# Routed attention: scatters two at a time behind each tile's weighing, TensorE's part as a loop, GpSimd filling the ring of rows

## The reference, cut to what matters

```python
x = x + tanh(g_xattn[3]) * L3_xattn(layernorm(x), ctx, ctx, Wq, bq, Wk, bk, Wv, bv, Wo, bo)
x = x + tanh(g_ffn[3]) * L3_ffn(layernorm(x), router_w, w1, b1, w2, b2)

def L3_ffn(x, router_w, w1, b1, w2, b2):          # 8 experts, two for each token
    router_probs = softmax(x_flat @ router_w.T)
    top_k_probs, top_k_idx = lax.top_k(router_probs, TOP_K)
    top_k_probs = top_k_probs / (top_k_probs.sum(-1, keepdims=True) + 1e-08)
    cw = (one_hot(top_k_idx, E) * top_k_probs[..., None]).sum(axis=1)
    for e in range(E):
        output += cw[:, e:e+1] * (new_gelu(x_flat @ w1[e].T + b1[e]) @ w2[e].T + b2[e])
```

## Time and profile before

| | us |
|---|---|
| median of the timed runs | 3279.86 (3278.26 to 3281.05) |
| the profiled execution, its own time | 3298.21 |
| its span in the profile | 3296.4 |
| TensorE busy | 2532.8 (77%) |
| VectorE busy | 1566.6 (48%) |
| ScalarE busy | 1380.2 (42%) |
| GpSimd busy | 978.3 (30%) |

### The profile page before, as it was taken

How to read it: one execution, slowest core, us unless ns; L and a number is a source line. 1 busy time by engine, 2 the same in 40 slices (tenths; PEclk the granted TensorE clock), 3 DMA queues, 4 the chain that set the end, 5 groups by cost and what they waited for, 6 DMA issues and landing times. The chain is left out here.

```text
span 3296.4 us, 74894 instructions
## 1 busy us (share of the span) xinstructions
PE 2532.8 (77%) x28202; PEld 1794.6 (54%) x28202; DVE 1566.6 (48%) x4283; ACT 1380.2 (42%) x1992; POOL 978.3 (30%) x1052
## 2 busy tenths in 40 slices
PE   4888864439997799989999969993288777358883
PEld 2555543328886455567777735551145444247773
DVE  3555544424443577622222247776667665513322
ACT  2555533213332466644545436661055444124441
POOL 4444426634444112110000000001112433634444
PEclk9999976669999899989999979996599888679997
DMA  3010101126665222100000011110011111146666
GB/s 98 22 24 20 23 16 38 39 80 195 197 192 153 78 53 61 34 3 0 0 0 0 1 44 45 41 41 11 11 32 31 37 35 37 44 144 191 189 186 219
DMA packets 143775, 219.56 MB, mean 67 GB/s; under 512 B 27177, under 2 KB 94513, under 8 KB 143026
## 3 DMA queue, kind: packets, MB, share of 16 engines
q1 hardware_dynamic: 96930, 90.25, 10.8%
q10 hardware_dynamic: 29232, 90.37, 8.8%
q0 software_dynamic: 17408, 36.21, 3.2%
HBM read 157.48 MB, written 43.61 MB: 61 GB/s over the span
## 5 line engine op out<-in xcount | busy, mean ns | idle before, releaser
L1541 DVE TENSOR_REDUCE mx<-psS 128x16 f32<-128x1024 f32 x264 | 322.6, 1222 | 321.9 <-PE psS L1096 294.1
L650 POOL DMA_INDIRECT yg<-ysb,yidx x288 | 279.5, 970 | 421.0 <-DVE ysb L2005 190.6
L470 POOL TENSOR_TENSOR ve<-mv,eps 128x4 f32<-128x4 f32 x102 | 20.3, 199 | 1184.4 <-DVE mv L1517 1182.3
L756 ACT ACTIVATE work<-psT 128x1024 f32<-128x1024 f32 x260 | 266.2, 1024 | 215.5 <-PE psT L1105 214.8
L750 ACT ACTIVATE work<-work 128x1024 f32<-128x1024 f32 x264 | 278.3, 1054 | 135.9 <-DVE work L1543 132.7
L1096 PE MATMUL psS<-kexp,qT 64*64 64x512 f32 x2112 | 307.6, 634 | 31.0 <-DMA kexp<-kT 15.3
L1543 DVE TENSOR_TENSOR work<-psS,mx 128x1024 f32<-128x1024 f32 x264 | 323.2, 1224 | 9.1
L1105 PEld LDWEIGHTS psT<-ident,work 128*128 128x128 f32 x2080 | 239.6, 145 | 151.5 <-issue 99.8
L1105 PE MATMUL psT<-ident,work 128*128 128x128 f32 x2080 | 288.3, 283 | 5.3 <-ACT work L756 3.3
L1381 PEld LDWEIGHTS psY<-w_ffn,work 128*128 128x128 f32 x2016 | 247.8, 192 | 9.4 <-DVE work L1976 1.2
L1381 PE MATMUL psY<-w_ffn,work 128*128 128x128 f32 x2016 | 248.5, 275 | 1.6 <-DVE ysb L1999 1.0
(11 more groups left out here) (278 smaller groups left out, 4645.0 us busy)
## 6 DMA issues: line engine op xcount, KB each, us to landing
w_ffn<-in_wmoe ACTq DMA_DIRECT2D x72, 578.0 KB
w_ffn<-in_wmoe ACTq DMA_DIRECT2D x72, 576.0 KB
ctxT<-in_ctxT SPq DMA_DIRECT2D x76, 256.0 KB, 2.8
xin<-xg SPq DMA_DIRECT2D x144, 132.0 KB
kexp<-kT SPq DMA_DIRECT2D x1152, 16.0 KB
gio<-yg SPq DMA_DIRECT2D x16, 512.0 KB, 3.9
work<-yg SPq DMA_DIRECT2D x16, 512.0 KB, 6.4
yg<-ysb,yidx POOLq DMA_INDIRECT x288
```

The lines of the kernel that those rows point to most:

```text
L650: e.indirect_dma_start(out=yg, out_offset=bass.IndirectOffsetOnAxis(ap=yidx[:, b, t:t + 1], axis=0), in_=ysb[:, b, t, :], in_offset=None, ...
L756: e.activation(pT[:, s % 2, :], psT[:, :], ACT.Copy).then_inc(pt_ok, 1)
L1541: e.tensor_reduce(mx[:, :], src, AX, ALU.max).then_inc(s_max, 1)
```

## The change

Three things in `attention_routed(3)`, and what they need elsewhere:

- GpSimd's `scatter(k)` issues two indirect DMAs in place of eight; k runs from 0 to 63. One such pair is issued behind each tile's weighing: `behind_weighing(u, s)` waits for `pv_ps` of tile (u, s). After the last turn the remaining 27 pairs follow in two runs, with the last two norms and fills between them.
- `rows(c)`, new on GpSimd, writes the normalised rows to `ring`. VectorE's `apply` writes the same numbers to a new tile `xnf` of one chunk, from which TensorE transposes. `macc` is one buffer, and VectorE waits for `rank_ps` before it updates it.
- TensorE's program has turns 0 to 3 written out, then a loop of five passes of two turns, then six turns. Its waits take their values from the loop's register where they are inside.

```diff
-                def scatter(g, c):
-                    if c == 0:
+                def rows(c):
+                    b = (c % 2) * LT
+                    if c >= 8 and c % 2 == 0:
+                        e.wait_ge(m[f"sd{c // 2 % 4}"], 16 * 2 * GT * (c // 8))
+                    e.wait_ge(m["rstd"], c + 1)
+                    for t in range(LT):
+                        mm = e.tensor_scalar(ring[c // 2 % 4][:, b + t, 0:D], xs(None, c, t), mmv[:, b + t, 0:1],
+                                             mrstd[:, 1, b + t:b + t + 1], ALU.subtract, ALU.mult)
+                    mm.then_inc(m["nrm"], 1)
+
+                def scatter(k):
+                    g, c, t0 = k // 8, k // 4 % 2, 2 * (k % 4)
+                    if k % 8 == 0:
                         e.wait_ge(m["seq"], MSTEPS[lay] * (g + 1))
-                    for t in range(GT):
+                        e.wait_ge(m["nrm"], 2 * g + 2)
+                    for t in range(t0, t0 + 2):
                         e.indirect_dma_start(
...
+                def behind_weighing(u, s):
+                    k = 4 * (u - 6) + s - 3
+                    if k >= 0:
+                        e.wait_ge(pv_ps, K0 + lay * TILES + u * LT + s + 1)
+                        scatter(k)
...
-                for u in range(CHUNKS + 5):
+                for u in range(CHUNKS):
+                    behind_weighing(u, 0)
                     if u + 2 <= CHUNKS:
                         ln(ATT[lay], None, u + 2)
-                    if 2 <= u < CHUNKS + 2:
+                    if u >= 2:
                         norm(u - 2)
-                    if u < CHUNKS:
-                        x_bias(lay, None, u)
-                    if u >= 6 and u % 2 == 0:
-                        scatter((u - 6) // 2, 0)
-                    if u >= 7 and u % 2 == 1:
-                        scatter((u - 7) // 2, 1)
-                scatter(NG - 1, 1)
+                    x_bias(lay, None, u)
+                    behind_weighing(u, 1)
+                    if u >= 2:
+                        rows(u - 2)
+                    behind_weighing(u, 2)
+                    behind_weighing(u, 3)
+                first = 4 * (CHUNKS - 6) - 3
+                norm(CHUNKS - 2)
+                rows(CHUNKS - 2)
+                for k in range(first, 8 * (NG - 3)):
+                    scatter(k)
+                norm(CHUNKS - 1)
+                rows(CHUNKS - 1)
+                for k in range(8 * (NG - 3), 8 * NG):
+                    scatter(k)
...
-                        mm = e.transpose(psX[:, t * P:(t + 1) * P], ring[c // 2 % 4][:, c % 2 * LT + t, 0:D], ident[:, :])
+                        mm = e.transpose(psX[:, t * P:(t + 1) * P], xnf[:, t, :], ident[:, :])
...
-                for u in range(CHUNKS + 4):
+
+                def turn(i, u):
...
+                for u in range(4):
+                    turn(None, u)
+                with e.Fori(0, (CHUNKS - 6) // 2) as i:
+                    turn(i, 4)
+                    turn(i, 5)
+                for u in range(CHUNKS - 2, CHUNKS + 4):
+                    turn(None, u)
...
                     if c >= 2:
                         e.wait_ge(m["xn"], c - 1)
+                        e.wait_ge(m["nrm"], c - 1)
...
                 def apply(c):
                     b = c % 2 * LT
-                    if c >= 8 and c % 2 == 0:
-                        e.wait_ge(m[f"sd{c // 2 % 4}"], 16 * 2 * GT * (c // 8))
+                    if c >= 1:
+                        e.wait_ge(m["xt_ps"], c)
...
-                        mm = e.tensor_scalar(ring[c // 2 % 4][:, b + t, 0:D], xs(None, c, t), mmv[:, b + t, 0:1],
+                        mm = e.tensor_scalar(xnf[:, t, :], xs(None, c, t), mmv[:, b + t, 0:1],
...
-                    step(e.tensor_tensor, macc[:, lay // 3, (g + 1) % 2, :], macc[:, lay // 3, g % 2, :], mcol[:, 8, :], ALU.add)
+                    e.wait_ge(m["rank_ps"], g + 1)
+                    step(e.tensor_tensor, macc[:, lay // 3, 0, :], macc[:, lay // 3, 0, :], mcol[:, 8, :], ALU.add)
```

More of the change, by code:

```diff
@@ L140, in program @@
         ring.append(gio3[:, :, :])
+        xnf = sb("xnf", [P, LT, D])
         lgt = sb("lgt", [P, GT * E])
@@ L1189, in attention_routed, with turn_x, route @@
                 m = MO[lay]
-                def turn_x(c):
-                    e.wait_ge(m["xn"], c + 1)
-                    e.wait_ge(x_up, K0 + lay * CHUNKS + c + 2 if c + 2 <= CHUNKS else K0 + (lay + 1) * CHUNKS)
+                def turn_x(i, u):
+                    e.wait_ge(m["xn"], val(i, u, 1, -2))
+                    e.wait_ge(x_up, val(i, min(u, CHUNKS + 1), 1, K0 + lay * CHUNKS - 1))
                     for t in range(LT):
-                        mm = e.transpose(psX[:, t * P:(t + 1) * P], ring[c // 2 % 4][:, c % 2 * LT + t, 0:D], ident[:, :])
+                        mm = e.transpose(psX[:, t * P:(t + 1) * P], xnf[:, t, :], ident[:, :])
                     mm.then_inc(m["xt_ps"], 1)
-                def route(c):
-                    e.wait_ge(m["xt_sb"], c + 1)
+                def route(i, u):
+                    e.wait_ge(m["xt_sb"], val(i, u, 1, -2))
                     for t in range(LT):
@@ L1202, in route, with group, rank @@
                     mm.then_inc(m["r_ps"], 1)
-                def rank(g):
-                    e.wait_ge(m["seq"], MSTEPS[lay] * g + 18)
+                def group(i, u, per, plus):
+                    return per * ((u - 5) // 2) + plus if i is None else i * per + (per * ((u - 5) // 2) + plus)
+                def rank(i, u):
+                    e.wait_ge(m["seq"], group(i, u, MSTEPS[lay], 18))
                     out8 = psX[:, GT * E:2 * GT * E].rearrange("p (t x) -> p t x", t=GT)
@@ L1210, in rank @@
                                  start=False, stop=False, skip_group_check=True)
-                    e.matmul(out8, ones16[:, :], macc[:, lay // 3, g % 2, :].rearrange("p (a x) -> p a x", a=1)
+                    e.matmul(out8, ones16[:, :], macc[:, lay // 3, 0, :].rearrange("p (a x) -> p a x", a=1)
                              .broadcast_to([P, GT, E]), start=False, stop=True).then_inc(m["rank_ps"], 1)
@@ L1224, in attention_routed @@
                 p_turn(lay, None, 0, 0)
-                for u in range(CHUNKS + 4):
+                def turn(i, u):
                     inside = u < CHUNKS
-                    c = u - 3
+                    routed = 3 <= u < CHUNKS + 3
+                    ranked = u >= 5 and u % 2 == 1
                     for s in range(LT):
                         if inside:
-                            scores(lay, None, *ahead(u, s, 2))
+                            scores(lay, i, *ahead(u, s, 2))
                         if s == 1 and inside:
[L1232 to L1240, removed]
+                            q_proj(lay, i, u + 1)
+                        if s == 1 and routed:
+                            turn_x(i, u)
+                        if s == 2 and routed:
+                            route(i, u)
+                        if s == 3 and routed:
+                            e.wait_ge(m["lg"], val(i, u, 1, -2))
+                        if s == 3 and ranked:
+                            rank(i, u)
@@ L1241, in attention_routed @@
                         if inside:
-                            p_turn(lay, None, *ahead(u, s, 1))
-                        if s == 3 and u >= 5 and u % 2 == 1:
-                            e.wait_ge(m["rk"], (u - 5) // 2 + 1)
+                            p_turn(lay, i, *ahead(u, s, 1))
+                        if s == 3 and ranked:
+                            e.wait_ge(m["rk"], group(i, u, 1, 1))
                         if s == 3 and u + 2 <= CHUNKS:
-                            ln_t(ATT[lay], None, u + 2)
+                            ln_t(ATT[lay], i, u + 2)
@@ L1247, in attention_routed @@
                         if inside:
-                            weigh(lay, None, u, s)
+                            weigh(lay, i, u, s)
                         if s == 0 and inside:
-                            v_proj(lay, None, u + 1)
+                            v_proj(lay, i, u + 1)
                         if s == 2 and inside:
-                            k_proj(lay, None, u + 2)
+                            k_proj(lay, i, u + 2)
                         if s == 3 and 0 < u <= CHUNKS:
-                            out_proj(lay, None, u - 1)
+                            out_proj(lay, i, u - 1)
@@ L1255, in attention_routed @@
+                for u in range(4):
[5 more added lines that the diff above has]
+                    turn(None, u)
                 e.wait_ge(m["seq"], MSTEPS[lay] * (NG - 1) + 20)
-                e.matmul(psO[:, 0:E], ones16[:, :], macc[:, lay // 3, NG % 2, :], start=True, stop=True).then_inc(m["cnt_ps"], 1)
+                e.matmul(psO[:, 0:E], ones16[:, :], macc[:, lay // 3, 0, :], start=True, stop=True).then_inc(m["cnt_ps"], 1)
```

## The result

The changed kernel takes 3239.9 us (median of four runs, 3236.2 to 3244.3) and the kernel before 3279.1 beside it; the ratio is 0.9887 (95% interval 0.9864 to 0.9909). It is faster, by about 40 us where 75 were forecast. Its profiled execution took 3239.0 us, 59.2 less than the profiled one of before. I read the changed kernel's stretches first, cut as in the earlier trace rows: a turn without scatters (u = 4), the ten turns u = 6 to 15, of these u = 11, 12 and 15 by themselves, and the tail. Columns: us, then busy us (instructions) of TensorE, its weight loads, VectorE, ScalarE and GpSimd, granted clock, DMA share, GB/s.

The account below looks back on a forecast made before the run. In turns u = 6 to 15, TensorE was taken to finish late while runs of scatters are under way. Terms: -85.4 + 10 = -75.4 us, so 3298.2 becomes 3222.8 profiled, less 18.3 for the median: 3204 us, range 3185 to 3285.

Parts of the forecast that it names:

- Scatters in pairs: Turns u = 6 to 15: pairs win back the 95.4 us lost, less 0.25 us for each of 40 pairs: -85.4 us.
- Do the pairs keep apart: GpSimd's queue per turn: one pair alone, three with gaps of 0 to 2 us; waiting costs nothing.
- GpSimd fills the ring: Routed turns: four fills of 0.45 us each, 1.8 per turn, hidden under TensorE; 0 us in the ten turns.
- One `macc`, the loop, code blocks: VectorE's wait for `rank_ps`, TensorE's loop and its fewer fetched code blocks in layer 3's routed attention: 0 us each.
- The tail: After the last `normalise`: 54 scatters remain instead of 48, with two fills; 78.9 against 68.8 us, +10 us.
- From the profile to the median: Whole kernel: the timed median lies 18.3 us below the profiled execution, so 3222.8 becomes 3204 us.
- the stage's shares: Layer 3's routed attention, roughly 2500 to 2900 us: TensorE's share by slices read as 9, then 7 and 6.
- Rival B: Ten turns: half the loss stays because three of four pairs lie close; -47.7 + 10, 3242 us; chance 0.18.
- Rival C: Ten turns: each pair opens its own late window; 3299 us, slower from 2.1 us per pair; chance 0.15.
- D: TensorE's loop: each pass fetches about five code blocks again, 13.5 us per pass, 68 in all; 3272 us; chance 0.04.

Follow-up runs that it names:

- pairs only: Kernel before with only GpSimd's scatters in pairs (turns unrolled, VectorE fills the ring, two macc buffers): 3217.9 us, ratio 0.9799 to before.
- VectorE's fill: Changed kernel with the ring filled by VectorE instead of GpSimd, pairs and loop kept: 3210.4 us (0.9785); in the set with before at 3212.7 us, 3187.8 us (0.9923).
- the unrolled kernel: Changed kernel with TensorE's loop written out again, pairs and GpSimd's fill kept: 3237.6 us, ratio 0.9862 to before.
- the worst kernel: Changed kernel with scatters back in runs of eight, loop, one macc and GpSimd's fill kept: 3292.9 us, ratio 1.0035 to before.
- the best: Changed kernel with the ring filled by VectorE, pairs and loop kept, in the set with before at 3212.7 us: 3187.8 us, ratio 0.9923.

## Why the prediction was wrong

By its own steps:

- **Scatters in pairs, -85.4 us: right.** Alone they take the ten turns from 304.5 to 225.1, -79.4. Left of the loss are 16.0 us over 209.1. The ten turns hold 37 pairs, as my own sum for the tail has it (k = 37 is the first one left), and not the 40 that I took here, so it is 0.43 per pair where I took 0.25. On a 3212 chip nothing is left (208.1).
- **Do the pairs keep apart: right for the order, and closeness wasn't the price.** `ln` waits for VectorE (3.6 us in the turn shown above) and holds up the second pair, as I said. In the changed kernel the fill then parts it from the third, and the two turns in which the third and the fourth pair do join are its shortest.
- **GpSimd fills the ring, 0 us: this is the step that failed.** The price was 0.80 us each, within my bounds but not the 0.45 that I took. The error was to count GpSimd's own time only (15.8 of 20.9 us: hidden). The fill costs 16.2 us in the ten turns on the 3280 chip (241.3 against 225.1 for pairs only; 15.8 against VectorE's fill) and 4.7 on the other (212.9 against 208.1). It slows the very steps that TensorE waits for: the wait for `mask` is 1.9 to 2.2 us in the changed kernel and 1.5 with VectorE's fill on a 3280 chip. So what costs is the fill's place, which the term didn't ask for: behind the fourth pair the same fill costs the ten turns nothing that can be seen (219.8).
- **One `macc`, the loop, code blocks: 0, right.** No block on q8 between 2525 and 2710, and 5 in all ten turns, where about half of the 25 was forecast.
- **The tail, +10: 13.6.** The 3.6 too much are mostly the fills': 6.4 us for two instead of 3.6.
- **From the profile to the median, -18.3 us: failed too.** The profiled execution of before was 18.3 us above its median, and I took the same off the changed kernel's. Its own lay 0.9 below its median. Between 8 and all of the 18 lay in stages that the change doesn't touch: by so much is that one profile longer outside the ten turns and the tail than the nine others from 3280 chips.

The sum: the ten turns came out 22.2 us longer than forecast (6.0 pairs, 16.2 fill), the tail 3.5, and the rest 9.6 shorter: 3239.0 in place of 3222.8. With the 19.2 us of the last step that is the whole miss of 36. Of the earlier trace rows I read the stage's shares wrong as well: they are 8, then 7, then 3, not 9, 7 and 6; no term hangs on them.

Rival B gave 3242 us, 2 from what was measured, by luck: it kept 47.7 us of the stall for the closeness of the pairs, while all that is left with pairs alone is 16 us. Rival C falls (0.43 us a pair, far from 2.1), and D falls with the unrolled kernel.

Open: why TensorE is late beside scatters on some chips and not on others. The context loads weren't slower there: they take 2.7 us from issue to landing in both traces of the kernel before, and a scatter takes GpSimd 0.97 us in both; how long a scatter takes to land, no view of these turns shows. It isn't the fetching of code. Open too is how the fill's 16.2 us add up. Of the 4.7 us of the 3212 chip, 4.1 are TensorE's longer waits for `mask` (5.9 us in u = 7 to 13 against 1.8). Of the rest a large part is the granted clock: the share of the clock that is lacking, times the length of the turn, adds up over the ten to some 10 us for the changed kernel and 1.6 for pairs only, so by this estimate at most about 9 us come from there. Why it falls behind one wait of 2.2 us and not behind another was not found. Scatters of fewer rows, which would tell issuing from moving, weren't tried, since rows left unwritten make the experts' stage race.

## What to carry to other kernels

Give work to an idle engine only after asking what it does to its neighbour's steps on the critical path and to what is queued behind it; its own busy time says nothing of that. Cut long runs of GpSimd's DMAs into pairs between TensorE's work; how close the pairs then stand mattered less here than what else stood between them. Put a forecast against the median only after asking which stages made the profiled execution longer than it.

## What the runs showed of the hardware that I had not expected

The same program differs by 2.1% between sets on different chips (3279.9 and 3212.7 us), and all of it lies in the turns in which GpSimd scatters while TensorE works: 304.5 and 237.0 us. An edit's worth differs with it, 1.1% and 0.3% here. A stretch in which TensorE is held up has a second price: behind 7.1 us in which it was busy for 3.9, the granted clock was 0.50; in the worst kernel the same matmuls kept it busy for 238 us and in the best for 184. Waits of 2.2 us were enough for the same fall in two turns, and one of 2.2 and one of 1.9 us were not. And GpSimd's 128x128 `tensor_scalar` takes 0.78 to 0.83 us.
